# Loading the gate and up weights of a transformer feed-forward block two tiles ahead instead of one

## The reference

```python
# _layernorm: (x - mean) / sqrt(var + 1e-5), no weights
x = _layernorm(x + _L0_attn_ref(x, ...))
g = jnp.einsum('th,ih->ti', xf, gate_w) * gate_s      # gate_w 5632 x 2048
u = jnp.einsum('th,ih->ti', xf, up_w) * up_s          # up_w   5632 x 2048
hdn = jax.nn.silu(g) * u
out = jnp.einsum('ti,hi->th', hdn, down_w) * down_s   # down_w 2048 x 5632
x = _layernorm(x + out)
```

## Time and profile before

| | us |
|---|---|
| two runs without a profile | 5450.45 and 5546.64, median 5498.54 |
| profiled execution, slowest core | 5371.21 |
| its span (first to last instruction) | 5369.4, the slowest of 8 cores (5329.6 to 5369.4) |
| feed-forward part of this span | from about 3060 to the end |
| PE busy over the span | 3844.1 (72%) |
| DVE, ACT, POOL busy | 1913.8, 1610.3, 332.2 |
| read from HBM | 652.01 MB |

### The profile page before, as it was taken

How to read it: one execution, slowest core, us unless ns; L and a number is a source line. 1 busy time by engine, 2 the same in 40 slices (tenths; PEclk the granted TensorE clock), 3 DMA queues, 4 the chain that set the end, 5 groups by cost and what they waited for, 6 DMA issues and landing times.

```text
span 5369.4 us, 67555 instructions; the slowest of 8 cores (5329.6 to 5369.4 us)
## 1 busy us (share of the span) xinstructions
PE 3844.1 (72%) x20400; PEld 1828.4 (34%) x20400; DVE 1913.8 (36%) x4134; ACT 1610.3 (30%) x3184; POOL 332.2 (6%) x581
## 2 busy tenths in 40 slices
PE   0466667666666666666377699877999599859986
PEld 0233223223333333333133244433444244424443
DVE  2222223444444444444133333233332333233323
ACT  0111100024555455555210133223332233223322
POOL 0000000000000000000000011111111111101111
PEclk9877788878788888887688799998999799989998
DMA  4211121000000000000511299767987598759875
GB/s 123 59 32 36 30 74 56 14 13 9 5 9 5 11 5 9 5 5 1 141 47 40 74 280 281 254 198 244 289 270 246 183 276 276 244 183 290 271 251 177
DMA packets 207283, 673.46 MB, mean 125 GB/s; under 512 B 30240, under 2 KB 30752, under 8 KB 202848
## 3 DMA queue, kind: packets, MB, share of 16 engines
q1 hardware_dynamic: 120528, 340.64, 20.7%
q0 software_dynamic: 78928, 310.68, 18.1%
q10 hardware_dynamic: 7488, 17.83, 1.2%
HBM read 652.01 MB, written 16.78 MB: 125 GB/s over the span
## 4 chain that ended last, share of the span: by engine, by line
PE 37%; DMA 32%; DVE 12%; issue 10%; ACT 8%; DVEq 1%; SPq 0%; ACTq 0%; POOL 0%; POOLq 0%
DMA stg_gp<-up_l 19%; PE pD L1175 6%; PE pPT L584 6%; DMA stg_gp<-down_c 5%; PE pOP L964 5%; PE pQA L494 4%; ACT Ebuf L869 3%; PE pO L818 3%; ACT PTsb L841 3%; PE pPT L834 2%; DVE ubf L244 2%; PE pS L781 2%; DMA stage<-ow_l 2%; PE pS L792 2%; DVE stats L799 2%
## 5 line engine op out<-in xcount | busy, mean ns | idle before, releaser
L1095 PE MATMUL pG<-OX,gbf 128*128 128x512 bf16 x2816 | 644.6, 382 | 130.6 <-ACT gbf L235 130.6
L1104 PE MATMUL pU<-OX,ubf 128*128 128x512 bf16 x2816 | 654.9, 387 | 113.0 <-DVE ubf L244 111.4
L1175 PE MATMUL pD<-h_fm,dbf 128*128 128x512 bf16 x2816 | 634.1, 381 | 79.3 <-DVE dbf L244 75.0
L244 DVE CAST ubf<-stg_gp 128x1024 bf16<-128x1024 f32 x352 | 244.5, 695 | 860.8 <-DMA stg_gp<-up_l 836.8
L818 PE MATMUL pO<-PTsb,vtm 128*128 128x128 bf16 x2176 | 240.1, 240 | 314.2 <-ACT PTsb L841 308.2
L1104 PEld LDWEIGHTS pU<-OX,ubf 128*128 128x128 bf16 x2816 | 272.5, 99 | 482.5 <-issue 187.5
L1095 PEld LDWEIGHTS pG<-OX,gbf 128*128 128x128 bf16 x2816 | 277.1, 99 | 469.1 <-issue 142.6
L1175 PEld LDWEIGHTS pD<-h_fm,dbf 128*128 128x128 bf16 x2816 | 272.2, 98 | 419.5 <-issue 119.3
L841 ACT CAST PTsb<-pPT 128x512 bf16<-128x512 f32 (+3 forms) x640 | 313.1, 525 | 270.1 <-PE pPT L834 269.7
L1117 ACT ACTIVATE sig<-pG,gates_sb 128x512 bf16<-128x512 f32 x176 | 120.9, 687 | 866.2 <-DVE tmid L1122 581.6
L869 ACT ACTIVATE Ebuf<-pS,stats 128x512 bf16<-128x512 f32 (+3 forms) x512 | 314.3, 621 | 207.3 <-DVE stats L860 202.4
(11 more groups left out here) (133 smaller groups left out, 3738.1 us busy)
## 6 DMA issues: line engine op xcount, KB each, us to landing
stg_gp<-up_l POOLq DMA_DIRECT2D x352, 512.0 KB, 6.1
stg_sy<-gate_l SPq DMA_DIRECT2D x352, 512.0 KB, 6.4
stg_sy<-down_c SPq DMA_DIRECT2D x128, 512.0 KB, 6.0
stg_gp<-down_c POOLq DMA_DIRECT2D x128, 512.0 KB, 5.1
stg_sy<-down_c SPq DMA_DIRECT2D x64, 384.0 KB, 7.0
stg_gp<-down_c POOLq DMA_DIRECT2D x64, 384.0 KB, 4.4
stage<-x SPq DMA_DIRECT2D x64, 256.0 KB, 3.4
xst<-x POOLq DMA_DIRECT2D x16, 1024.0 KB, 6.1
```

The lines of the kernel that those rows point to most:

```text
L244: e.tensor_copy(d[:, a:a + cc], tiles[i][:, 0:cc]), inc=cP)
L1095: P.op("tensor", lambda e, wi=wi, d=d, gc0=gc0: e.matmul(pG[wi][:], gbf[wi][:, d * 128:(d + 1) * 128], OX[:, d * S + gc0:d * S + gc0 + 512 ...
L1104: P.op("tensor", lambda e, wi=wi, d=d, gc0=gc0: e.matmul(pU[wi][:], ubf[wi][:, d * 128:(d + 1) * 128], OX[:, d * S + gc0:d * S + gc0 + 512 ...
L1175: P.op("tensor", lambda e, di=di, hh=hh, jj=jj, ii=ii: e.matmul(pD[di][:], dbf[hh][:, jj * 128:(jj + 1) * 128], h_fm[:, ii * 512:(ii + 1) ...
```

## The change

`gu_loads` is defined once ahead of the group loop. Tiles 0 and 1 are loaded before the first group; inside an iteration `ii` the call is for tile `ii + 2` instead of `ii + 1`; and tiles 0 and 1 of the next group are loaded right after the last iteration of this group, ahead of the down stage. Neither buffers nor staging slots are added.

```diff
+            pre2 = {0: gu_loads(0), 1: gu_loads(1)}
             for grp in range(NGRP):
                 gc0 = grp * 512
-                def gu_loads(ii):
-                    ...
-                pre = gu_loads(0)
                 P.w("tensor", vE, a4_done_v)
                 P.wf("tensor", h_free)
                 for ii in range(IC):
                     wi = ii % 2
-                    g_ready, u_ready = pre
+                    g_ready, u_ready = pre2.pop(ii)
...
                     ubf_free[wi] = (tMM, u_mm)
-                    if ii + 1 < IC:
-                        pre = gu_loads(ii + 1)
+                    if ii + 2 < IC:
+                        pre2[ii + 2] = gu_loads(ii + 2)
                     P.w("scalar", tMM, g_mm)
...
                 h_ready = vE.n
+                if grp + 1 < NGRP:
+                    pre2[0] = gu_loads(0)
+                    pre2[1] = gu_loads(1)
                 def down_loads(do):
```

More of the change, by code:

```diff
@@ L1074, in build_program, with gu_loads @@
             HALF = IC // 2
+            def gu_loads(ii):
+                wi = ii % 2
+                P.wf("scalar", gbf_free[wi])
+                g_ready = lc_sy(gate_l[ii], gbf[wi], 0, D)
+                P.wf("vector", ubf_free[wi])
+                u_ready = lc_gp(up_l[ii], ubf[wi], 0, D)
+                return g_ready, u_ready
+            pre2 = {0: gu_loads(0), 1: gu_loads(1)}
             for grp in range(NGRP):
                 gc0 = grp * 512
-                def gu_loads(ii):
-                    wi = ii % 2
-                    P.wf("scalar", gbf_free[wi])
-                    g_ready = lc_sy(gate_l[ii], gbf[wi], 0, D)
-                    P.wf("vector", ubf_free[wi])
-                    u_ready = lc_gp(up_l[ii], ubf[wi], 0, D)
-                    return g_ready, u_ready
-                pre = gu_loads(0)
                 P.w("tensor", vE, a4_done_v)
```

## The result

| | before | after |
|---|---|---|
| median of the runs without a profile, us | 5448.02 (10 runs, 5346.87 to 5546.64) | 5495.63 (11 runs, 5466.47 to 5617.8) |
| profiled execution, us | 5371.21 | 5480.06 |
| its span, us | 5369.4 | 5478.2 (8 cores: 5441.4 to 5478.2) |

The ratio is 1.0225, interval 1.0164 to 1.0286: the change made the kernel slower, and whether by more than 2% the interval leaves open. The forecast was +13 us, at most 2% either way with a chance of 0.88; measured is 0.0225 x 5371 = +121 us (88 to 154).

The account below looks back on a forecast made before the run. It took the gp path, which brings the up tiles through the GpSimd queue, to bound the kernel. +15 + 43.5 - 45.4 = +13 us: 5384 on the profiled 5371.2, 5463 on the unprofiled 5450.5; range 5345 to 5575.

Parts of the forecast that it names:

- The gp path sets the pace: Gate and up stage: up tiles arriving through the GpSimd queue, not the number of buffers, limit it, at 7.56 us a tile.
- As long as the gp path sets the pace, this costs nothing per iteration: Inside a group: TensorE waits ahead of G instead of ahead of U, at the same 7.56 us.
- The end of the stage, +3.8 four times: End of each gate and up stage: tmid, G and U follow the last up cast, +15 us over four groups.
- Ahead of the down stage, +14.5 three times: Before three down stages: two up tiles loaded first delay the first down tile's second half, +43.5 us in all.
- Start of groups 1 to 3, -15.1 three times: Group starts: two tiles already lie in the buffers, so the gp path brings two fewer, -45.4 us in all.
- The lost cover, +124: Rival, inside a group: TensorE's lateness feeds back through up buffers, late tiles paid twice, +111, with the 13 +124; chance 0.15.
- a pace beyond 8.1: Sign in the gate and up stage that would decide for the slower rival: pace above 8.1 us a tile.
- The gate loads get out of the up loads' way, -100 at best: Rival, gate and up stage: later gate DMAs let up pieces land sooner, pace 6.91 at best, some -100 us; chance 0.12.

Follow-up runs that it names:

- e3: Changed kernel without loads ahead of the down stage, only the up tile loaded and cast early, gate cast behind sig as before: ratio 1.0024, pace 7.59 us.
- e7: Changed kernel, orders kept, SyncE's gate DMAs held until the h_fm behind the up cast: ratio 1.0104, pace 7.80 us.
- e10: Kernel before, cast orders kept, SyncE's gate DMAs made to wait for up casts: no ratio; cores 4 to 7 took 5632.6 to 5642.5 us, pace 9.20.
- e11: Kernel before, cast orders kept, gate DMAs held until the h_fm behind the up cast: ratio 1.0123, pace 7.81 us.
- e1: Changed kernel with the call for tile ii + 2 moved behind h_fm(ii), loads ahead of the down stage kept: ratio 0.9953.
- e6: Kernel before with each iteration's sigmoid computed three times on ACT: ratio 1.007, pace 7.77 us.
- e12: Kernel before, cast orders kept, gate DMAs held until the tmid behind the up cast: ratio 1.0321, pace 8.56 us.

## Why the prediction was wrong

Point by point, as it put them:

- *The gp path sets the pace.* Right, before and after. DVE's waits for a landing are the largest wait of DVE in both.
- *"As long as the gp path sets the pace, this costs nothing per iteration: ... at the same 7.56 us."* This is the step that failed. The wait did move ahead of G, and that by itself is free (e3). But the sentence took the gp path's own speed as given. The same move on ACT put the gate casts ahead of `sig` and, through them, the gate DMAs among the up DMAs (e7, e10 and e11 show that it is the DMAs). The up path is limited by how long its pieces take to land, and that rose by up to 0.67 us. 0.64 x 176 = 113 us, nearly all of the miss.
- *The end of the stage, +3.8 four times.* Held: 7.9 us instead of 3.9 in group 0.
- *Ahead of the down stage, +14.5 three times.* Held: 23.5 us behind the last U block in group 0, 21 to 24 in groups 0 to 2 (core 4), and 7.2 in group 3, which loads nothing ahead.
- *Start of groups 1 to 3, -15.1 three times.* Held: tile 2 lands when tile 0 did, and the wait ahead of G(2) is 42.8 us. That these two terms cancel is shown by e1, which has both and the old order.
- *The lost cover, +124.* Its size was met almost exactly, and so was the sign that it had named (a pace beyond 8.1), both by chance. Its mechanism was the feedback through the up buffers. DVE's waits for a buffer did rise, from 23.9 to 50.0 us, but 26 us in all is small beside 113, and with the up cast early alone (e3) the time didn't change.
- *The gate loads get out of the up loads' way, -100 at best.* The right resource with the wrong sign. I had reckoned that the gate casts come some 4 us later against the up casts and so move away from them. The gate DMAs do come 3.2 us later in the round. But in the kernel before they were already behind both up DMAs, the best place found in any run; the change moved them into the middle, ahead of the second up half. (The case was also said to pass 2%; its -100 us is 1.9% of 5371.) What I had left out is the chain that kept them there: gate cast behind `sig`, `sig` behind the `tmid` of the iteration ahead, `tmid` behind the cast of the second up half. The trace had it, in the waits of the kernel before:

```profile
ACT sig L1117 <- DVE tmid L1122: 581.6, 114, 8.4
```

  I had left it out, as idle time of an engine that nobody waits for. It was the wait that timed the DMAs.

What stays open: why both gate pieces 3.5 and 4.5 us behind (e6, +0.24) cost as much as both 1.0 and 1.5 us behind (e11, +0.28); what decides at the engines which of two queues is served; and how the 0.43 us by which the first half is held after divides between waits for the buffer and DVE's other work. Whether a third staging slot for the up path would take the price away was not tried.

## What to carry to other kernels

When a change moves an instruction that frees a staging buffer, ask when the DMA behind it now goes out, and against which other DMA: at a DMA share of 0.87 to 0.91, as here, that phase can cost more than the waits that the change was about. A slot's round (cast to issue, landing, held) adds up to the pace, and each part can be read from the trace; forecast all three, the landing too. An engine's idle time is harmless, but it may be what holds a competing transfer back, so a wait that looks free may be worth keeping.

## What was unexpected in the hardware

- The time in which a 512 KB piece lands depends on when the other queue's pieces were issued: 6.2 us with the gate pieces 1.9 and 2.8 us behind, 6.5 with them 1.0 and 1.5 behind, 6.9 with them 2 to 3 us ahead (after), 7.2 with them 0.2 and 0.7 behind, 7.8 with one about 0.5 us ahead and one at the same time. The load is no guide: the same bytes spread over the longest time (a pace of 9.2 us) have the longest landing. The Trainium skill (DMA: Bandwidth & Descriptors, Queues, rings and completion order) says that each DMA engine takes turns, a packet at a time, between the queues that it has work for. The packets agree in part: in e12 two queues moved 0.36 and 0.30 MB in the same 3 us, but in e10 the gate queue alone moved data for 4.5 us after the up piece's issue. Whether the up piece was ready for the engines in that time is not told by the profile.
- Two queues released by the same instruction don't start together. In e10 SyncE's issue started 0.08 us after the cast's end (3302.36 to 3302.44) and GpSimd's 0.56 us after it (3302.92). And in e12 GpSimd's issue started 0.19 us ahead of SyncE's, and SyncE's packets came first. An additional wait meant to put one DMA behind the other put it ahead.
